# Adding up gathered expert rows behind the next-but-one batch's layer norm, in a fused two-layer transformer kernel

## The reference

```python
h = layernorm(x) * (1 + ca) + sa
x = x + ga * attn_topk(h)         # 16 heads of 16, causal, softmax over the 32 largest scores of a row
h = layernorm(x) * (1 + cb) + sb
x = x + gb * moe_top1(h)          # 8 dense experts of 256 x 256, relu, gate = softmax maximum
h = layernorm(x) * (1 + ca) + sa  # ca, sa, ... of the second layer from here
x = x + ga * attn_wide(h)         # 16 heads of 64, causal
h = layernorm(x) * (1 + cb) + sb
y = h + attn_narrow(layernorm(h) * ln1_w)   # 16 heads of 16, causal
n = layernorm(y) * ln2_w
rw, sel = top2(softmax(n @ router_w));  rw = rw / rw.sum()
y = y + sum_k rw[k] * (gelu(n @ w1[sel[k]]) @ w2[sel[k]])   # 8 experts, 256 -> 512 -> 256
x = x + gb * y
```

## Time and profile before

| | us |
|---|---|
| median of 3 runs (lowest, highest) | 6084.94 (6066.3, 6086.87) |
| the profiled execution | 6095.92, its span 6094.1 |
| busy PE, PEld, DVE, ACT, POOL | 4532.7, 2900.3, 4101.1, 2745.6, 1902.9 |
| mean granted TensorE clock | 0.853 of full speed |

### The profile page before, as it was taken

One profiled execution on the slowest core, in us unless ns is written; L12 is line 12 of the kernel. 1 busy time (PEld: TensorE's weight loads), 2 busy tenths in 40 slices (PEclk: granted clock), 3 DMA queues, 4 the chain that ended last, 5 costly groups with the idle time before them and its releaser, 6 DMA issues. The chain is left out here.

```text
span 6094.1 us, 83316 instructions
## 1 busy us (share of the span) xinstructions
PE 4532.7 (74%) x30341; PEld 2900.3 (48%) x30341; DVE 4101.1 (67%) x8455; ACT 2745.6 (45%) x6035; POOL 1902.9 (31%) x1563
## 2 busy tenths in 40 slices
PE   4454488888676858888777658888777586999776
PEld 2333345666333535566533444666533353566334
DVE  6999956777885656777787655777778665322630
ACT  2434315665343623666344441666435360455333
POOL 2565603343323321333322440334333331000001
PEclk7666689999797979999888778999878797999888
DMA  3000001000212020000311111000020211000312
GB/s 120 11 11 25 1 21 29 15 12 12 51 17 89 30 83 22 15 12 9 61 17 62 46 61 51 15 12 12 15 53 12 88 39 41 17 10 9 61 60 71
DMA packets 113333, 213.59 MB, mean 35 GB/s; under 512 B 25728, under 2 KB 70632, under 8 KB 109552
## 3 DMA queue, kind: packets, MB, share of 16 engines
q1 hardware_dynamic: 104736, 190.94, 11.5%
q0 software_dynamic: 6144, 16.79, 0.9%
q10 hardware_dynamic: 2048, 0.53, 0.0%
HBM read 154.38 MB, written 49.73 MB: 33 GB/s over the span
## 5 line engine op out<-in xcount | busy, mean ns | idle before, releaser
L1499 DVE MAX8 vals<-work 128x8 f32<-128x128 f32 (+7 forms) x1536 | 1080.3, 743 | 0.4
L467 PE MATMUL ring<-ident,pr 128*128 128x128 f32 x2304 | 485.1, 331 | 534.0 <-POOL pr L1873 483.6
L1868 POOL TENSOR_SCALAR keep<-ssb,vals 128x128 bf16<-128x128 f32 (+7 forms) x512 | 875.2, 1721 | 0.0
L1855 POOL TENSOR_TENSOR pool_step<-ones 128x2 f32<-128x2 f32 x256 | 49.6, 194 | 2256.7 <-DVE vals L1499 2255.9
L1513 DVE MATCH_REPLACE8 work<-vals,work 128x128 f32<-128x128 f32 (+7 forms) x1024 | 750.7, 739 | 0.0
L574 PE MATMUL pA<-SC 128*128 128x512 f32 (+3 forms) x1536 | 634.4, 524 | 138.0 <-ACT SC L1208 113.0
L467 PEld LDWEIGHTS ring<-ident,pr 128*128 128x128 f32 x2304 | 331.6, 169 | 685.7 <-POOL pr L1873 510.3
L1873 POOL TENSOR_TENSOR pr<-keep,pr 128x128 f32<-128x128 bf16 (+7 forms) x512 | 647.0, 1285 | 0.0
L1147 ACT ACTIVATE prT<-ring 128x512 f32<-128x512 f32 (+1 forms) x768 | 381.0, 497 | 540.5 <-PE ring L467 532.6
L1628 DVE TENSOR_REDUCE nmax<-pA 128x1 f32<-128x1024 f32 (+7 forms) x512 | 382.1, 750 | 270.9 <-PE pA L575 259.8
L1499 DVE MAX8 vals<-ssb 128x8 f32<-128x128 f32 (+7 forms) x512 | 362.8, 749 | 291.0 <-ACT ssb L1135 271.3
(11 more groups left out here) (224 smaller groups left out, 8281.4 us busy)
## 6 DMA issues: line engine op xcount, KB each, us to landing
SC<-in_w SPq DMA_DIRECT2D x64, 512.0 KB, 7.2
stage<-parts SPq DMA_DIRECT2D x384, 64.0 KB, 2.4
parts<-SC SPq DMA_DIRECT2D x72, 256.0 KB, 2.4
SC<-parts SPq DMA_DIRECT2D x144, 128.0 KB, 7.9
SC<-in_wqkv SPq DMA_DIRECT2D x32, 384.0 KB, 2.9
rows_out<-SC SPq DMA_DIRECT2D x92, 128.0 KB, 1.7
SC<-rows_in SPq DMA_DIRECT2D x20, 512.0 KB, 3.9
SC<-in_ffn_we SPq DMA_DIRECT2D x4, 2048.0 KB, 10.2
```

The source lines that it names most:

```text
L467: mm = pe.transpose(r[:, blk % 4 * P:blk % 4 * P + P], pr0[:, p % 2, blk * P:blk * P + P], ident[:, :])
L1499: m = v.max(vals0[:, y, i, 8 * n:8 * n + 8], src[:, lo:hi])
L1868: pool.tensor_scalar(keep0[:, lo:hi], ssb0[:, p % 2, lo:hi], vals0[:, p % 2, i, TOPK - 1:TOPK], None, ALU.is_ge).then_inc(s["k"], 1)
```

## The change

The sum (DVE's four parts, L1750 to L1764) becomes a function of its own, `collect`. For batches 0 and 1 DVE runs it in the prelude of batch b+2, between the layer norm "n0" and `project_narrow`; for batches 2 and 3 it stays right behind `moe`. POOL computes that norm's inverse deviations (`norm("n0", b + 2)`) between the eighth and the ninth gather, where before it did so behind the sixteenth. The stage "collect" of the ticks is gone on all engines; its share goes, with a third of that of "route", to "wide" and "moe". `G` moves from the start of `SC` to columns 14336 to 18431.

```diff
-    STAGES = (("wide", 8 * 17, 0.49), ("prep", 12, 0.04), ("flip", 8 + 48, 0.22), ("route", 6, 0.06),
-              ("moe", 23, 0.13), ("collect", 6, 0.06))
+    STAGES = (("wide", 8 * 17, 0.51), ("prep", 12, 0.04), ("flip", 8 + 48, 0.22), ("route", 6, 0.04),
+              ("moe", 23, 0.19))
...
-        G = cut(0, 2 * NT * D).rearrange("p (i d) -> p i d", d=D)
+        G = cut(14336, 2 * NT * D).rearrange("p (i d) -> p i d", d=D)
...
# moe() of PE, SP and ACT, each at its end:
-                for i in range(6):
-                    at("collect", i)
...
# DVE
                 for j in range(SM.TILES):
                     at("moe", j)
-                for i in range(6):
-                    at("collect", i)
+
+            def collect(b):
+
                 for q in range(4):
                     v.wait_ge(m1["ga%d" % q], (b + 1) * 64)
...
             def prelude(b):
                 v.wait_ge(s_xl, b * 16 + 16)
                 norm("n0", b, XL)
+                if b >= 2:
+                    collect(b - 2)
                 project_narrow(0, b, vall0, lambda name, i: None)
                 ch.restart()
...
                 moe(b, at)
+                if b + 2 >= B:
+                    collect(b)
...
# POOL
                 for i in range(2 * NT):
+                    if i == NT and b + 2 < B:
+                        norm("n0", b + 2)
                     pool.indirect_dma_start(out=G[:, i, :], out_offset=None, in_=ys_dram,
...
-                for i in range(6):
-                    at("collect", i)
-
...
-                if b + 1 < B:
-                    norm("n0", b + 1)
+                if b == 0:
+                    norm("n0", 1)
```

## The result

The changed kernel takes 6034.03 us (median of five runs, 6024.63 to 6037.85) against 6084.94 (6066.3 to 6086.87): 51 us less, ratio 0.9919, 95% interval 0.9900 to 0.9938. The profiled execution's span is 6035.3 us against 6094.1. The forecast was 100 us less. The sign was right and so was the place of the gain; one cost, that of the ticks in the tile loop, was much larger than I made it.

The account below looks back on a forecast made before the run. TensorE was taken to bound the tile loop and wide attention, with idle stretches at batch changes and routing. Terms -137.7 + 57 - 48 + 29 gave about -100 us, so 5985 us for the median, range 5930 to 6042.

Parts of the forecast that it names:

- batch changes: Between one batch's last expert matmul and the next norm: 51.8 us saved at each of two, 34.1 at the third, -137.7.
- tile loop: Expert tile loop: 28 more ticks cost +19 us a loop, bounds +12 and +65; times three, +57.
- routing: Routing stage: 9 ticks fewer, one selection less behind the scatters, -16 us a batch; times three, -48.
- wide, prep, flip: Wide attention +6.7 us for ten more ticks, flip +3 for a spread and reciprocal, prep unchanged; times three, +29.
- elsewhere: Projections, feed-forward and batch 3 were to stay as they are, 0 us.
- 1 us to spare: First two batch changes: the sum ends at 2178.5, DVE is next wanted for the first subtraction at 2179.4; cost nothing.
- a sign of being wrong: Behind the batch change: the forecast counts as wrong if the first subtraction waits for the additions.
- Port rule: Batch change: DVE's eight normalisations would hold GpSimd's gathers up to 2.8 us, losing 1.9 at each of two; total -96.
- My price for the added work: Tile loop: PE's 12.1 us at clock 0.62 and 3.64 at 0.5 become 9.7 at the loop's 0.96.
- rival (a): Tile loop: the selection chain, not PE, sets the pace; loop gains 65 us instead of 19, total +38, slower; 7%.
- The base: Whole kernel: the profiled execution lies 11 us above the median of three runs, so 5996 becomes 5985.

Follow-up runs that it names:

- e6: Changed kernel with three throwaway matmuls into an unused PSUM bank ahead of each tile's ticks, batches 0 to 2; 6018.7 us, ratio 0.9892 to before.
- e3_wide: Changed kernel with the tile loop's tick share back at 0.13 and wide's raised to 0.57; 5988.19 us, ratio 0.983 to before.
- e11: e3_wide with the expert tiles' Gelu replaced by a plain copy, leaving the gelu out of the result; 5948.51 us, ratio 0.9768 to before.
- e9: Kernel before with the expert tiles' Gelu replaced by a plain copy, leaving the gelu out of the result; 6043.04 us, ratio 0.9922 to before.
- e5: Changed kernel with the expert tiles' Gelu replaced by a plain copy, leaving the gelu out of the result; 5947.36 us, ratio 0.9778 to before.
- e10: e3_wide with three throwaway matmuls ahead of each tile's ticks; 6001.85 us, ratio 0.9856 to before.

## Why the prediction was wrong

Sums over the three batches with ticks, from the stage marks; forecast and measured:

```
batch changes     -137.7   -136.3   (-50.3, -50.2, -35.8)
tile loop         +57      +99.3    (+34.9, +32.4, +32.0)
routing           -48      -37.8
wide, prep, flip  +29      +18.6    (wide 18.3, prep 14.2, flip -15.2, behind it 1.3)
elsewhere          0       -2.5
all               -100     -58.7    (spans: -58.8)
```

- **Batch changes: right to 2 us, partly by luck.** The chain (gathers, norm at the eighth, the sum beside the projections) came out within 2 us at each point, and X and the row broadcasts were in time. But the sum was not hidden with 1 us to spare: it held the first subtraction back by 2.0 us, which I had named as a sign of being wrong. I had taken PE's pace behind the transposes from before; its matmuls of L433 took 14.0 us instead of 15.8, and that hid the delay. The 3 us that L442 gained at the lower clock stood in no term; the transposes, 1.8 us earlier than forecast, paid for part of it.
- **Port rule: not confirmed at that size.** The gather beside the eight normalisations took 1.14 us instead of 0.95, and those beside DVE's two-input operations up to 1.22. The gathers were not held for 2.8 us, and the sum ended at T + 30.9, where I had T + 31.9 without such a hold.
- **Tile loop: the term that failed.** I forecast +19 a loop; it was +33, and the 42 us of excess over three loops are the whole miss, the other terms nearly cancelling. Without table loads it is 149.2 - 129.3 = 19.9 in batch 1 (21.5 in the others), close to my figure. The other 12.5 us of batch 1 are the loads: 21 instead of 18, each costing the loop 1.34 instead of 0.87 us. My price for the added work, 9.7 us of PE at the loop's 0.96, was low: PE's busy time times clock is 149.76 x 0.91 = 136.3 after and 128.7 x 0.96 = 123.6 before, 12.7 more, or 13.2 at 0.96. Of batch 1's 32.4 us these are 13.2; 7.8 are the lower clock (149.8 - 136.3/0.96), and 11.4 are added idle time of PE (27.6 instead of 16.3), where I had 4.8. What I did not foresee is that ACT's hand-overs, which the loop before bore at 0.96, make PE wait longer when four ticks instead of three follow each tile, and that the clock is then lower. ACT was busy 102.6 of the 146 us, more than DVE, and stands in no step of my sum. I had taken the clock of the loop as given and scaled to it, and had looked at DVE's load (rival (a)) where ACT's order decided. Rival (a) did not come: of PE's idle time there 2.7 us go back to DVE (the reciprocal) and nothing to GpSimd's selections.
- **Routing: right in kind.** Three selections stood behind the scatters instead of four, and 12.6 us went, not 16.
- **Wide and flip.** Wide +6.1 a batch, forecast 6.7. Prep and flip moved by +4.7 and -5.1, probably since what shifts by nine ticks shifts work out of one into the other; I had +3.
- **The base.** The profiled execution of before was 11 us above its median, that of after 3 us above; the spans differ by 58.8 us, the medians by 51.

Shown by taking away: the loads' 28.2, 15.7 and 10.9 us, and that the sum has no part in the loop. Only argued from rows: that the clock falls because of the pauses (e6 raises it by 0.03 and points there, no more), and that a load costs more in the changed loop because its ticks are denser (they are also other ticks; no run varied density alone).

## What to carry to other kernels

Price work that is moved into a busy loop by the hand-overs it adds on the second busiest engine, and not only by its busy time on the first: here PE's work cost 13 us a loop where 10 were forecast, and ACT's table loads, hidden by a third in the loops with 62 ticks, cost their full length in the one with 90. A cheap way to see this ahead is one run with the loop's activation function replaced by a copy. Idle time between stages can be emptied by moving work out, but then ask where it lands: taken out of the tile loop the 28 ticks gave 42 us back and cost wide 30, and with what routing and flip did besides, e3_wide gained about twice what the change did.

## What the runs showed of the hardware that was not expected

In the loops of batch 1 a table load of 1283 ns cost 0.84 and 0.87 us with 62 ticks beside the tiles (e11, e9) and 1.34 with 90 (e5). With 21 loads gone the loop's granted clock was 0.98 instead of 0.91, and 92 of its matmuls took 7.6 us less. Filling PE's pauses with throwaway work went with a clock higher by 0.03 and cost that loop nothing (e6); at a clock of 0.99 it cost the loop 6.4 us (e10). A stand of 2.8 us before 32 matmuls went with a clock of 0.70 and 3.0 us more for them in one run, and with 1.00 and nothing in another (after, e3_wide). The gathers' issue was stretched by 0.2 to 0.3 us beside DVE's work, not blocked for its length.
